# The second batch's windowed attention begun earlier, value products in runs, and an order from measured durations

## The reference, cut to what matters

```python
x = layernorm(x + L0_attn(x))   # rotary, softmax over the last 64 keys (allowed = (j <= i) & (i - j < 64))
x = layernorm(x + L0_ffn(x))    # r * (relu(xk @ W_k.T)**2 @ W_v.T), r a sigmoid, with a token shift
x = layernorm(x + L1_attn(x))   # linear attention: elu(q)+1, elu(k)+1, random features, no softmax
x = layernorm(x + L1_ffn(x))    # a block: layernorm, causal rotary softmax attention, layernorm,
                                # a mixture of 8 experts (top 2, a capacity), both with residuals
```

## Time and profile before

| | us |
|---|---|
| three runs | 2046.11, 2048.51, 2050.54; median 2048.51 |
| span of the profiled execution | 2046.3 |
| PE busy | 1785.6 |
| DVE, ACT, POOL busy | 1026.1, 899.2, 826.0 |

### The profile page before, as it was taken

How to read it: one execution, slowest core, us unless ns; L and a number is a source line. 1 busy time by engine, 2 the same in 40 slices (tenths; PEclk the granted TensorE clock), 3 DMA queues, 4 the chain that set the end, 5 groups by cost and what they waited for, 6 DMA issues and landing times. The chain is left out here.

```text
span 2046.3 us, 33038 instructions
## 1 busy us (share of the span) xinstructions
PE 1785.6 (87%) x10804; PEld 1077.4 (53%) x10804; DVE 1026.1 (50%) x2373; ACT 899.2 (44%) x1855; POOL 826.0 (40%) x1247
## 2 busy tenths in 40 slices
PE   4889668999999979999989999999709999999980
PEld 2557445556546645545655644444406666666660
DVE  2556444876746877575678777776410000111115
ACT  2454324375665537476444656566403222222212
POOL 4552346442247563224747324322452334433220
PEclk9899889999999999999999999999859999999995
DMA  5600155212144503124540314131141333333115
GB/s 159 93 10 1 41 84 74 33 32 32 63 63 64 105 2 49 15 64 66 90 76 2 56 50 58 19 52 64 42 131 28 72 80 82 82 78 80 23 18 172
DMA packets 92019, 123.12 MB, mean 60 GB/s; under 512 B 14049, under 2 KB 62113, under 8 KB 91697
## 3 DMA queue, kind: packets, MB, share of 16 engines
q1 hardware_dynamic: 77520, 104.19, 25.3%
q0 software_dynamic: 14336, 16.83, 4.9%
HBM read 44.65 MB, written 25.56 MB: 34 GB/s over the span
## 5 line engine op out<-in xcount | busy, mean ns | idle before, releaser
L968 ACT ACTIVATE b_probs<-b_psum 128x512 f32<-128x512 f32 (+3 forms) x896 | 430.7, 548 | 254.7 <-PE b_psum L839 235.6
L1213 DVE TENSOR_REDUCE b_mneg<-b_psum 128x2 f32<-128x384 f32 (+5 forms) x608 | 338.8, 593 | 150.4 <-PE b_psum L826 138.0
L1304 POOL TENSOR_SCALAR_AFFINE_SELECT b_probs<-b_probs 128x512 f32<-128x512 f32 (+1 forms) x400 | 239.6, 610 | 318.8 <-ACT b_probs L968 308.0
L826 PE MATMUL b_psum<-b_qk 96*128 96x192 bf16 (+4 forms) x1280 | 307.8, 300 | 6.0 <-DVE b_before L1185 1.7
L839 PE MATMUL b_psum<-b_qk 99*128 99x192 bf16 (+5 forms) x1344 | 279.4, 291 | 23.6 <-DMA b_qk<-b_mrow 9.2
L854 PE MATMUL b_psum<-b_probs,b_v 128*32 128x192 f32 (+4 forms) x2688 | 235.0, 425 | 8.5 <-issue 5.3
L1589 DVE TENSOR_TENSOR b_ye<-b_psum,b_b2b 128x512 f32<-128x512 f32 x32 | 22.1, 692 | 428.8 <-PE b_psum L1544 428.8
L1568 ACT ACTIVATE b_hid<-b_psum,b_b 128x512 f32<-128x512 f32 x128 | 87.9, 687 | 318.1 <-PE b_psum L1535 316.0
L1544 PE MATMUL b_psum<-b_w,b_hid 128*128 128x256 f32 x1024 | 222.4, 379 | 0.8 <-ACT b_hid L1568 0.8
L1535 PE MATMUL b_psum<-b_xgt,b_w 128*128 128x512 f32 x512 | 221.8, 594 | 0.0
L1497 POOL DMA_INDIRECT before_last_norm<-b_ye,b_ids x64 | 99.5, 1555 | 300.8 <-DMA before_last_norm<-b_ye,b_ids 164.5
(11 more groups left out here) (206 smaller groups left out, 2444.5 us busy)
## 6 DMA issues: line engine op xcount, KB each, us to landing
b_qk<-b_split SPq DMA_DIRECT2D x372, 128.0 KB, 5.0
b_w<-in_W SPq DMA_DIRECT2D x16, 1024.0 KB
b_src<-in_x SPq DMA_DIRECT2D x4, 1024.0 KB, 5.8
before_last_norm<-b_early SPq DMA_DIRECT2D x4, 1024.0 KB, 4.8
b_o<-before_last_norm SPq DMA_DIRECT2D x4, 1024.0 KB, 5.3
before_last_norm<-b_o SPq DMA_DIRECT2D x4, 1024.0 KB
normed<-b_y SPq DMA_DIRECT2D x4, 1024.0 KB
b_rows<-before_last_norm SPq DMA_DIRECT2D x8, 512.0 KB, 7.7
```

The source lines that it names most:

```text
L826: ins = pe.matmul(out[:, i, :], q[0:KS, h, P * t:P * t + P], q[0:KS, HG + h, a:e], start=not last, stop=True, skip_group_check=True)
L968: act.activation(probs_of((g, h2, t))[:, heads[0]:heads[-1] + 1, a - BANK * h2:e - BANK * h2], bank, ACT.Exp, scale=SCALE).then_inc(s.exp_ ...
L1213: dve.tensor_reduce(out, in_bank(("max",) + x[1:], heads, e - a), AX.X, ALU.max, negate=True).then_inc(s.max_read, 1)
L1304: ins = pool.affine_select(out=block, in_=block, pattern=[[0, HG], [1 if ahead else -1, z - y]], compare_op=ALU.is_ge, fill=none, base=y - ...
```

## The change

Five things change, and nothing of what is computed.

One: batch 1 (`EARLY`). Its rows are loaded in `set_up` into `y`, which far attention fills only later (the tables that lay there for a moment go to `o`), on a semaphore of their own. `fetch` reads `y`, `refill` writes `xt` and waits no longer for `out1`; its local `proj` reads `xt`, and its local result goes to `y`. In return `h_take` of batch 0 waits for batch 1's last local `proj`, `keep` and `o_take` of batch 1 wait for `out1` of batch 0, `y1` of batch 1 waits for `source`, and the first far `divide` of batch 0 waits until batch 1's result has been turned out of `y`. `ORDER` stays.

Two: the cells of a half form runs of two (three and two where there are five), and one `values` step does a run. `probs` becomes a ring of 1536 columns in which a cell takes its width; the space is free when the run that used it is done.

Three: `turn` does two tiles at once, in any of now six banks.

Four: `mparts` is wide enough that `rows` takes 128 stationary columns instead of 12.

Five: costs and delays of the scheduler are others, the longest chain counts delays between engines too.

```diff
-CELLS = 3
+RING_COLUMNS = 1536
+EARLY = 1
+    LATE = {"PE": 0.2, "DVE": 0.14, "ACT": 0.14, "POOL": 0.1}
-            urgent[x] = st.cost + max([urgent[y] for y in followers[x]], default=0)
+            urgent[x] = st.cost + max([urgent[y] + (0.0 if steps[y].engine == st.engine else self.LANDING[x[0]]
+                                                    if st.engine == "SP" else self.LATE[st.engine])
+                                       for y in followers[x]], default=self.AHEAD.get((x[0], x[-1]), 0.0))
...
-    BANKS = (0, 1, 2, 3, 7)
+    BANKS = (0, 1, 2, 3, 6, 7)
...
+    def xa_left(self, b):
+        return ("out1", 3, b - 1) if b == EARLY else self.last_projected(b, True)
...
+    def place_cells(self):
+        self.batches, self.batch_of, self.column, self.freed_by = {}, {}, {}, {}
+        at, held = 0, []
+        for g, h in self.units:
+            cells = self.query_cells(g, h)
+            sizes = (3, 2) if len(cells) == 5 else (2,) * (len(cells) // 2)
+            ends = [sum(sizes[:n + 1]) for n in range(len(sizes))]
+            for n, end in enumerate(ends):
+                self.batches[g, h, n] = cells[end - sizes[n]:end]
+                for t, a, e in self.batches[g, h, n]:
+                    if at + e - a > RING_COLUMNS:
+                        at = 0
+                    over = [x for x, y, z in held if y < at + e - a and z > at]
+                    held = [x for x in held if x[0] not in over]
+                    self.column[g, h, t], self.batch_of[g, h, t] = at, (g, h, n)
+                    self.freed_by[g, h, t] = self.batch_of[over[-1]] if over else None
+                    held.append(((g, h, t), at, at + e - a))
+                    at += e - a
...
-                    add(("fetch", y, c, b), "PE", 0.45, ("source", b), ("out1", 3, b - 1))
-                    add(("refill", y, c, b), "ACT", 0.6, ("fetch", y, c, b))
+                    add(("fetch", y, c, b), "PE", 0.435, *[] if b == EARLY else [("source", b), ("out1", 3, b - 1)])
+                    add(("refill", y, c, b), "ACT", 0.52, ("fetch", y, c, b))
...
-                add(("proj", j, t), "PE", 0.66, rows,
+                add(("proj", j, t), "PE", 1.29, rows,
...
-                ins = pe.transpose(rows_bank(x)[:, P * t:P * t + P], u.mparts[n % 2][:, t, :], u.id16[:, :])
+                ins = pe.transpose(rows_bank(x)[:, P * t:P * t + P], u.mparts[n % 2][:, 3 * HG * t:3 * HG * t + P], u.id16[:, :])
...
+                    for t, a, e in plan.batches[x[1:]]:
+                        cell = (g, h2, t)
+                        if plan.edges(cell, a, e):
+                            pe.wait_ge(s.cleared, order[("clear",) + cell] + 1)
+                        else:
+                            pe.wait_ge(s.exp_done, order[("power",) + cell + (plan.pieces(g, a, e)[-1],)] + 1)
+                        for h in range(HG):
+                            ins = pe.matmul(u.ot[32 * h:32 * h + 32, a:e], u.v[:, g % 4, t, (HD + 1) * h:(HD + 1) * h + 32],
+                                            probs_of(cell, a, e)[:, h, :], start=(t == t0), stop=True,
+                                            tile_position=(0, 32 * h), skip_group_check=True)
...
-                        if b:
-                            act.wait_ge(s.pj_ready, plan.projected(b - 1, False))
+                        act.wait_ge(s.pj_ready, plan.projected(b - 1, False) if b else plan.projected(EARLY, True))
...
+                    if not windowed[g] and not plan.place_of(g) and not b:
+                        done(dve, EARLY, "o_turn", 1)
+                        dve.wait_ge(s.back_ready, order[("back", plan.group_of(EARLY, True, 0), 1)] + 1)
...
+            sp.dma_start(u.y[:, :, :], a["x"][EARLY:EARLY + 1, :, :].rearrange("o (t p) d -> p (o t) d", p=P)).then_inc(early_in, 16)
             sp.wait_ge(loaded, 16 * (count + 3))
```

More of the change, by code:

```diff
@@ L147, in arrange @@
                     ready = max([done[y] + (0.0 if steps[y].engine == engine else self.LANDING[y[0]] if steps[y].engine == "SP"
-                                            else 0.12) for y in steps[x].after], default=0.0)
+                                            else self.LATE[steps[y].engine]) for y in steps[x].after], default=0.0)
                     if x[0] in self.TAKEN_BY:
@@ L170, in arrange @@
                     if x in issue_of:
-                        bank_free[self.bank[issue_of[x]]] = end + 0.12
+                        bank_free[self.bank[issue_of[x]]] = end + self.LATE[engine]
             if not moved:
@@ L195 @@
 class Plan(Planner):
-    BANKS = (0, 1, 2, 3, 7)
-    TAKEN_BY = {"proj": "store", "fetch": "refill", "max": "reduce", "rows": "lines", "exp": "power", "out": "divide",
+    BANKS = (0, 1, 2, 3, 6, 7)
+    TAKEN_BY = {"proj": "store", "fetch": "refill", "max": "reduce", "rows": "lines", "exp": "power", "out": "divide", "turn": "rest",
                 "back": "keep",
@@ L280, in describe @@
         turned, i = [], 0
[L281 removed]
+        self.place_cells()
         for b in range(1, B):
@@ L294, in prep @@
                 n = NT * j + t
-                add(("proj", j, t), "PE", 0.66, rows,
+                add(("proj", j, t), "PE", 1.29, rows,
                     name("load", 2 * j - 1, 1, 5, None) if t == 0 else None,
[L297 to L301, removed]
+                    self.final_values(2 * j - 3, 1) if j >= 2 else None)
+                add(("rotate", j, t), "DVE", 0.6, ("proj", j, t), name("add", *divmod(n - 2, NT)) if n >= 2 else None)
+                add(("store", j, t), "ACT", 0.2, ("rotate", j, t), self.final_values(2 * j - 3, 1) if j >= 2 else None)
+                add(("add", j, t), "POOL", 0.88, ("rotate", j, t), name("turn", *divmod(n // 2 - 1, 4)) if n >= 2 else None)
                 if t % 2:
@@ L337, in unit @@
             if h and not windowed[g]:
-                add(("least", g, h), "DVE", 0.28, last)
+                add(("least", g, h), "DVE", 0.1, last)
                 last = ("least", g, h)
@@ L341, in unit @@
                 name("rows", *before(mine, 2)) if before(mine, 2) else None)
-            add(("rows", g, h), "PE", 0.25, ("parts", g, h))
-            add(("lines", g, h), "ACT", 0.6, ("rows", g, h), name("spread", *before(mine, 2)) if before(mine, 2) else None)
+            add(("rows", g, h), "PE", 0.23, ("parts", g, h))
+            add(("lines", g, h), "ACT", 0.52, ("rows", g, h), name("spread", *before(mine, 2)) if before(mine, 2) else None)
             add(("spread", g, h), "SP", 0.5, ("lines", g, h))
@@ L439, in describe_layer @@
         for h in range(2):
-            add(("o_turn", h), "PE", 0.45, ("divide", near[-1], h))
-            add(("o_take", h), "ACT", 0.6, ("o_turn", h), self.last_projected(b, True))
+            add(("o_turn", h), "PE", 0.435, ("divide", near[-1], h))
+            add(("o_take", h), "ACT", 0.52, ("o_turn", h), other=[self.xa_left(b)])
         for k in range(4):
-            add(("pj", k), "PE", 1.75, ("o_take", k // 2), ("keep", near[0], k // 2))
-            add(("y1", k), "DVE", 1.55, ("pj", k))
+            add(("pj", k), "PE", 1.73, ("o_take", k // 2), ("keep", near[0], k // 2))
+            add(("y1", k), "DVE", 1.4, ("pj", k), other=[("source", b)] if b == EARLY else [])
         self.describe_norm(b, "n1", "y1", ("x1",))
@@ L547, in o_of @@
     def o_of(g):
-        return u.o if windowed[g] else u.y
+        return u.o if windowed[g] and plan.batch[g] != EARLY else u.y
     def in_bank(x, heads, w):
@@ L790, in _ @@
                             pe.wait_ge(s.fetched, 4 * b)
-                    x_rows = u.xa[:, :, 1:T + 1] if near else u.xt
+                    x_rows = u.xa[:, :, 1:T + 1] if near and b != EARLY else u.xt
                     for c in range(NC):
```

247 lines of the change are left out of this document (131 added, 116 removed).

## The result

| | before | after |
|---|---|---|
| median of four runs, us | 2047.31 | 1937.72 |
| lowest and highest | 2045.10, 2050.54 | 1937.11, 1945.39 |
| span of the profiled execution | 2046.3 | 1935.3 |

A forecast was written before the change was run, and what follows sets the result against it. PE was taken to set the time, 95% busy from 376 to 1465 us. Gains 52 + 4 + 37 + 4 = 97 gave span 1949, median 1951; own range 1925 to 1980, 8 in 10 from 1912 to 1999.

The forecast's parts named there:

- the fill before 131: Batch 0's local attention, 47.1 to 131 us: batch 1's first projection fills idle PE, gain 4 us, bounds 0 and 9.
- first maxima: At the start: last loads go some 5 us sooner, so the first maxima come earlier; gain 4 us, bounds 0 and 5.
- Part 1: 131 to 376 us: batch 1's local attention beside batch 0's layer closes PE's hole; gain 52 us, bounds 44 and 58.
- The 8% of idle time: PE's idle share assumed for the new stretch after 131 us, between 5% and 12%, giving 192.6 us against 245.0.
- Rival B: Batch 0's layer, 96 us, is drawn out; past 160 us half of the early batch's gain is lost: 1977, chance 0.10.
- Part 2: Values in runs and full-width rows save 46 us of PE work; 0.8 shows: 37 us, bounds 23 and 46.
- Rival A: Full stages: DVE and latencies take over, saved PE work becomes idle time, only the hole closes: 1984, chance 0.13.
- My sign for it: Test for runs and full-width rows: PE's busy time 45 us lower outside the clock's share.
- Part 3: Turns by two tiles, shared banks, ring, new order: 4 us at the start, otherwise 0, between -14 and +14.
- Rival D: The order fits better: idle after 376 halves (28 us), clock stays up (14 us): 1909, chance 0.13.
- C: Ring in runs: exponentials wait for whole runs, 101 us if ACT leads nowhere: 2052, or 2055 with lower clock; chance 0.04.
- wider weight loads: Full-width rows: 256 wider loads would add 25 us by the skill's rule if exposed; taken as 0 because they hide.

The follow-up runs named there:

- e3_noearly: The changed kernel without batch 1 begun early, its local attention again behind batch 0's layer: 1991.3 us.
- e1_single: The changed kernel with values in runs of one cell: 1945.4 us.
- e2_rows12: The changed kernel with rows on 12 stationary columns again: 1943.9 us.
- e4: The changed kernel with its order planned by the old durations, delays and chain rule: 1984.7 us.
- e7: The changed kernel with only the projection's planned duration put back, 0.66 for 1.29 us: 1961.7 us.
- e10: The changed kernel with turn in bank 6 alone, waiting for the rest before it, and all other steps in five banks: 1975.7 us.
- e11: The changed kernel with single-cell runs, three fixed places instead of the ring, and turn alone in bank 6, others in five banks: 1965.7 us.
- e9: The changed kernel with runs of one cell and the ring replaced by three fixed places of 512 columns: 1944.5 us.
- e5: The kernel before with only the scheduler's new durations, delays and chain rule: 2035.2 us.

## Why the prediction was right, point by point

The time held: 1937.7 lies in the forecast's own range, 13 us under the forecast. The parts did not all hold; two errors of opposite sign cancel, and that the sum came out so near is luck.

| term | forecast | measured | by |
|---|---|---|---|
| batch 1 early, with the fill before 131 | 52 + 4 | 54 | e3_noearly |
| runs | some 29 of the 37 | 8 (2 to 16) | e1_single |
| rows at full width | some 7 of the 37 | 6 (not clear of 0) | e2_rows12 |
| first maxima | 4 | 1.1 | marks above |
| order, sixth bank, ring | 0 (-14 to +14) | 12 to 47, 21 to 38, 0 | e4 to e7, e10, e11, e9 |

The measured parts depend on each other and must not be added: by undoing one at a time from after they make 54 + 8 + 6 + 47 + 38, 153 us for 110. As one path from before they do add: new durations 12 (e5), then the early batch, full-width rows, two-tile turns with single cells 69.5 (e11), then the shared bank 21 (e9), then the ring and runs 7 (after).

**Part 1** was right in size and mechanism. The 8% of idle time assumed for the new stretch are 20.4 of 245, 8.3%. Idle of over 3 us is one wait of 4.8 instead of none, and the clock is 0.95, 1.00 and 0.97, not 1.00 throughout. The fill before 131 is not to be seen as less idle time (11.7 us against 10.3 of the earlier trace rows). Rival B's beginning did happen: the layer, which B counts from 131, took 135 us (to 266.3) instead of 96. It stays under the 160 from which B decides, and PE didn't starve.

**Part 2** is the step that was mis-sized. The price of a switch was right (0.24 for 0.23), the count was right (153 for 160), and "how much of it shows" was wrong. I took 0.8 from DVE's tenths, holding that PE, busy 95% of the time from 376 to 1465, was the limit wherever DVE wasn't near its own. 8 of 36 showed for runs, 0.2, and at the upper end of the interval less than half. Being busy did not mean that PE was the limit there. In that stretch of before 55.1 us of waiting show as idle time; 27.4 more lie behind those gaps, and I estimate 24 at rows without a gap, as their time beyond that of the quicker rows of the same kinds. So PE waited for about a tenth of the stretch and not a twentieth. Rival A named the direction (what is saved becomes idle time), with the wrong engine: DVE is busy 72% from 376 to 1354 (701.42 of 978.00) and never became the bound. My sign for it, PE's busy time 45 us lower, was met (57.7) and told nothing: single cells, old durations and one bank fewer each add 20 us of busy time with the same instructions, so that drop belongs to no single part.

**Part 3** is the other one. "The old order already holds PE at 95%" was the same mistake, now on the low side: for order and bank I allowed a quarter of the visible idle time, 14 us. The durations and the bank also reach waits that don't show, 10.3 us of them in e4_oldcosts and 19.9 in e10_ownbank. Rival D, 42 us for an order that fits better, was nearest to the size of this part, at 0.13, but not in its terms. Idle time in the middle stretch is 38.0 us against 55.1, so 17 won and not 28. Its other term, 14 us of clock, did not come: the middle stands at 0.98 against 0.99. The ring was rightly put at nothing, and C's slack was there.

**The start** gave 1.1 instead of 4. The two waits of `turn` are gone, and the last `turn` before the maxima ends at 41.0 instead of 42.9; only 1.1 of these 1.9 us reach the maxima. The loads stand in SP's queue. SP's issues, before and after:

```profile
37.31 10.86 SPq L647 DMA_DIRECT2D b_qk<-b_split  x17
```

```profile
36.24 12.73 SPq L688 DMA_DIRECT2D b_qk<-b_split  x19
```

They begin 1.1 us sooner and then go at 0.64 and 0.67 us each, a train that the maxima wait for, still 5.05 us at 46.05. So the step that failed here is the 5 us by which I let the last loads go sooner.

The prediction also weighed wider weight loads, and took 0 for them. The rows of the loads for `rows` are 87 ns each with 12 columns (e2_rows12) and 100 with 128 (after), and PE's own steps show none of it, by the 0.003 us above. The Trainium skill, "TensorE: Matmul & The Clock Gate", section LDWEIGHTS, gives a load's time as the number of columns over 1.2, in ns, which would be 10 and 107. The rows agree for 128 columns and not for 12, and the measurement decides.

What stays open: in which sequence banks, readers and runs block each other, and whether the waits that take back what runs save come from the runs or from the order that the scheduler makes with them. A plan with the order held fixed would tell.

## What to carry to other kernels

Don't take an engine's busy share for the share of saved work that will show; count start-to-start distances, see how much of "busy" is waiting, and undo the part by itself. Before touching a tuned inner loop, put measured durations into the plan and see that no PSUM bank is kept for a step that is rarely there: here these two were worth more than the new form of the values. And measure such parts one at a time and together, for what is measured for a part can change sign (runs: -14 with the old durations, -10 with a bank fewer, +8 with both).

## What the runs showed of the hardware that I had not expected

Busy time of PE in the profile isn't a constant of the work: the same 10804 instructions show 1727.9 (after), 1748.1 (e4_oldcosts), 1748.7 (e10_ownbank) and 1739.6 us (e3_noearly) in four orders. By the table in part 2, 8.8 and 11.4 us of it are the lower clock in e4_oldcosts and e3_noearly; the rest of e4's and nearly all of e10's difference are waits. The Trainium skill, "Perfetto Trace Analysis", section "Tensor Engine Instruction (MATMUL, LD_WEIGHTS)", says that the end of such a row is an estimate and not an observation. The trace agrees, with rows of 0.33 us on an engine held for 0.17.

The clock fell for less time and cost nearly as much. The low stretches of after, their sums as in the earlier trace rows: three from 45.6 to 100.2, four from 151.4 to 369.8, seven from 625.8 to 1325.6:

```profile
sum 23.80, PE 19.38 PEld 12.95 DVE 11.17 ACT 2.99 POOL 4.20; mean PE 6.46 PEld 4.32 DVE 3.72 ACT 1.00 POOL 1.40
sum 17.00, PE 14.17 PEld 9.04 DVE 11.51 ACT 5.20 POOL 3.16; mean PE 3.54 PEld 2.26 DVE 2.88 ACT 1.30 POOL 0.79
sum 34.20, PE 31.00 PEld 19.84 DVE 23.93 ACT 12.55 POOL 10.71; mean PE 4.43 PEld 2.83 DVE 3.42 ACT 1.79 POOL 1.53
```

Behind 131 us, 51.2 us at the lower clock with 45.2 of work in them stand against 82.0 with 54.3 before: 31 us less of low clock, but only 9 less of slow work, since before the low time lay half in the hole. Over the whole span the lower clock stretches PE's columns by 34.9 us in after and 34.7 in before. And from 47.1 to 131 the clock is at 0.87 against 0.91, behind the same wait for the first maxima (5.05 and 4.3 us): that low stretch begins at 45.6 in after, but at 41.6 in before, so that 5.5 of its 10.3 us fall ahead of 47.1.
